# State cleared tile by tile, GpSimd scaling one tile in four, the flag and the loads in other places: one change to a graph network on one core

## The chip, the core and the metric

The kernel runs on one core of a Trainium2 chip. The core has five engines with queues of their own: TensorE (PE), VectorE (DVE), ScalarE (ACT), GpSimd (POOL) and SyncE (SP), and 16 DMA engines shared by the queues. The metric is the device time in microseconds of one execution, as the median of several.

## What is computed

A graph with N = 6250 nodes and E = 200,000 edges, sorted by target, 128 features. Two residual layers follow each other: a message network with sums by target, and an attention layer with a softmax by target.

```
edge_index = stack([src, dst])
h = maximum(layernorm(x), 0)
x = x + L0(h, edge_index, edge_attr)      # message network
h = maximum(layernorm(x), 0)
x = x + L1(h, edge_index)                 # attention

L0: m = relu(concat[h[src], h[dst], edge_attr] @ W1 + b1) @ W2 + b2
    agg = segment_sum(m, dst)
    u = relu(concat[h, agg] @ U1 + c1) @ U2 + c2
    return layernorm(h + u) * gamma + beta
L1: xl, xr = h @ Wl.T + bl, h @ Wr.T + br        (self loops added)
    e = att . leaky_relu(xl[src] + xr[dst])
    alpha = softmax of e over the edges of each target
    return elu(segment_sum(alpha * xl[src], dst) + bias)
```

## The kernel before

`gnn_program` runs the message network's edges (`edges_mlp`), a general middle part that is skipped in the fast case, and the attention (`edges_attention`). Both edge passes walk over 391 groups of 512 edges, 8 groups to a round, 49 rounds. For every group GpSimd issues four gathers (`gather_rounds`, L730) of 128 rows each from a table in memory: `tab_a` in the first pass, `tab_l` in the second. A ring of 8 group slots takes them, and a slot is free again when VectorE has added its rows (`m_sum`, L1286).

Ahead of the first pass stands the prelude (`prelude`). It loads the nodes `X` (49 tiles of 128 nodes), normalises them in 13 chunks of `CH` = 4 tiles (the last has one), and writes `tab_a`, the products of the normalised nodes with the first part of `W1`. The engines run in step `n` over the chunks:

- VectorE takes the statistics of chunk n (L578, L581) and makes the factors `rs` and `nm` of chunk n-1 (L610, L611).
- ScalarE takes the square root of chunk n (`sd`, L419), copies the turned chunk n-2 into `HT` (L423), scales chunk n-1 tile by tile into `xn`, whose buffer the profile calls m_attr_t (L431), and copies the products of chunk n-3 into the store buffer `at`, called m_pre (L438).
- TensorE turns chunk n-1 (L512) and multiplies chunk n-2 (L520).
- SyncE issues the loads, then the store of each chunk of `tab_a` (L375). There are two store buffers.

In between stands other work, hung to certain steps: GpSimd casts the edges' source and target rows (L476, L478) and reorders the target rows (`perm`, L480); TensorE turns them (`turn_rows`, L495) and VectorE takes them (`take_rows`, L567); `base` (L633) is the first target of each group's window of 32; four passes over 1568 columns and some short ones (L638 to L657) count whether the windows are as the fast path needs them; and TensorE and VectorE turn the count into `flag_i` (L551, L672). Every engine reads `flag_i` and branches (L706). GpSimd does so when all of `tab_a` and the zero rows at the tables' ends have landed, too. The products of the first five tiles for the target table `tab_b3` (L547 to L669) and their store (`store_early`, L384) are also part of the prelude; later tiles of it are made in the rounds, five ahead (`LEAD`).

The state `acc` holds 2 x 6304 sums per partition. In the rounds VectorE adds each group's window to it (L1295), and four slots into the round after the next the finished tile is used up (`tile(rnd, 2)`). `dve_tile`, `act_tile` and `pe_tile` hold this work of a round on nodes; `lead(rnd)` is the round's number up to 47.

## Time and profile before

| | us |
|---|---|
| median of 3 runs (lowest, highest) | 4053.22 (4052.76, 4057.73) |
| the profiled execution, its time | 4052.3 |
| the profiled execution, its span | 4050.5 |
| of its span busy: TensorE, VectorE | 3054.5, 2072.5 |
| of its span busy: ScalarE, GpSimd | 1780.8, 2983.4 |
| bytes moved by DMA | 455.98 MB |

The span is the stretch from the first to the last instruction that the profile shows. A row of the timeline tells an instruction's start, its length, its engine, its line, what it writes and reads, and in brackets how long the engine stood idle before it and what ended that. "issue" means that the profile shows nothing that was waited for. TensorE, weight load and matmul, has the names PEld and PE; a queue that issues DMAs has the name of its engine with a q.

### The profile page before, as it was taken

What the parts mean: (1) busy time and instruction counts of PE and PEld (TensorE: products, weight loads), DVE (VectorE), ACT (ScalarE), POOL (GpSimd) and SP (SyncE); (2) the same over time, 40 slices, a digit from 0 to 9 for tenths busy, and PEclk for the clock granted to TensorE, in tenths of its full rate; (3) what the DMA queues carried; (4) which work ended last, traced back from release to release, by engine and by line L of the source; (5) the groups of instructions that cost most, each with busy time, mean ns of one, the idle gap of its engine ahead of it and who ended that gap; (6) DMA issues with size and microseconds to landing.
All of it is one profiled execution on the core that took longest, in us unless ns stands there. A gap on an engine that the chain in (4) does not pass through costs nothing. (4 is left out here: it accounts for less than half of the span.)

```text
span 4050.5 us, 117915 instructions
## 1 busy us (share of the span) xinstructions
PE 3054.5 (75%) x30845; PEld 2211.2 (55%) x30845; DVE 2072.5 (51%) x7909; ACT 1780.8 (44%) x4395; POOL 2983.4 (74%) x3154
## 2 busy tenths in 40 slices
PE   4778878778887778788857777777777777777776
PEld 3667666666666666666634444444444444444444
DVE  5344444444444444444435555655565565556555
ACT  4333333333333333333335555555555555555555
POOL 4777777777777777777747777777777777777775
PEclk8777777877777777777768888888888888888887
DMA  6555555555555555555423333333333333333332
GB/s 163 144 145 139 145 142 143 144 141 140 143 146 137 146 141 145 138 146 137 121 65 86 85 86 85 85 85 86 85 85 85 86 86 85 85 85 86 85 85 58
DMA packets 397865, 455.98 MB, mean 113 GB/s; under 512 B 156453, under 2 KB 296963, under 8 KB 397791
## 3 DMA queue, kind: packets, MB, share of 16 engines
q1 hardware_dynamic: 297295, 249.90, 22.4%
q0 software_dynamic: 100096, 205.00, 20.4%
q8 instruction: 34, 0.56, 0.1%
q14 instruction: 40, 0.33, 0.0%
q10 hardware_dynamic: 400, 0.20, 0.0%
HBM read 434.70 MB, written 20.07 MB: 112 GB/s over the span
## 5 line engine op out<-in xcount | busy, mean ns | idle before, releaser
L730 POOL DMA_INDIRECT m_ring<-tab_a,m_idx x1564 | 1483.5, 949 | 516.5 <-issue 508.9
L730 POOL DMA_INDIRECT t_ring<-tab_l,t_idx x1564 | 1478.3, 945 | 517.1 <-issue 458.9
L1192 PE MATMUL bank<-w,m_attr_t 128*128 128x128 f32 x3128 | 733.5, 363 | 91.2 <-DVE m_hot L1276 91.0
L1909 PE MATMUL bank<-t_hot_t,t_win 96*128 96x128 bf16 x1564 | 329.3, 238 | 514.0 <-DMA t_ring<-tab_l,t_idx 506.2
L1192 PEld LDWEIGHTS bank<-w,m_attr_t 128*128 128x128 f32 x3128 | 629.6, 249 | 146.6 <-issue 107.2
L1241 ACT ACTIVATE m_hid<-m_pre 128x512 f32<-128x512 f32 x391 | 246.4, 630 | 999.9 <-DVE m_pre L1286 986.0
L1286 DVE TENSOR_TENSOR m_pre<-bank,m_ring 128x512 f32<-128x512 f32 x391 | 270.2, 691 | 784.2 <-DMA m_ring<-tab_a,m_idx 439.4
L1918 PE MATMUL bank<-t_zt,att_wn 128*128 128x512 f32 x782 | 545.4, 788 | 0.7 <-DVE t_zt L2018 0.7
L1960 ACT ACTIVATE t_z<-bank 128x512 f32<-128x512 f32 x391 | 233.5, 597 | 667.0 <-PE bank L1911 639.7
L1909 PEld LDWEIGHTS bank<-t_hot_t,t_win 96*128 96x128 bf16 x1564 | 166.3, 108 | 603.4 <-issue 581.2
L2062 DVE TENSOR_TENSOR t_old<-acc,t_shrink 128x64 f32<-128x64 f32 x391 | 88.3, 226 | 695.8 <-ACT t_shrink L1973 609.4
L1194 PE MATMUL bank<-m_win,m_hot_t 96*128 96x128 bf16 x1564 | 402.4, 257 | 0.0
L1928 PEld LDWEIGHTS bank<-t_a_edge,t_ring 128*32 128x32 f32 x12512 | 159.7, 126 | 421.7 <-issue 418.8
L1911 PE MATMUL bank<-ident,t_ring 128*128 128x128 f32 x1564 | 366.8, 311 | 0.0
L1954 ACT ACTIVATE t_a_edge<-bank 128x512 f32<-128x512 f32 x391 | 233.0, 596 | 237.6 <-PE bank L1899 227.7
L1183 PE MATMUL bank<-ident,m_ring 128*128 128x128 f32 x1564 | 306.8, 331 | 22.5 <-DMA m_win<-tab_b 22.5
L1236 ACT ACTIVATE m_attr_t<-bank 128x512 f32<-128x512 f32 x391 | 229.6, 587 | 156.5 <-PE bank L1183 155.2
L1966 ACT ACTIVATE t_a_row<-t_logit,t_den_max 128x512 f32<-128x512 f32 x391 | 278.5, 712 | 0.5 <-DVE t_den_max L2027 0.4
L1978 ACT ACTIVATE t_pen<-t_hot_t,t_big 128x512 f32<-128x512 bf16 x391 | 277.4, 710 | 0.0
L1899 PE MATMUL bank<-ident,t_a_row 128*128 128x128 f32 x1564 | 268.5, 299 | 10.8 <-ACT t_a_row L1966 2.0
L1202 PE MATMUL bank<-m_hid,m_hot 128*32 128x129 f32 x3128 | 193.6, 325 | 109.5 <-ACT m_hid L1241 69.8
L2018 DVE TENSOR_TENSOR t_zt<-bank,t_z 128x512 f32<-128x512 f32 x391 | 264.6, 677 | 11.9 <-ACT t_z L1960 11.9
(206 smaller groups left out, 5253.6 us busy)
## 6 DMA issues: line engine op xcount, KB each, us to landing
m_ring<-in_edge_attr_dram SPq DMA_DIRECT2D x390, 256.0 KB
m_row<-dst_rows SPq DMA_DIRECT2D x391, 128.0 KB
t_row<-dst_rows SPq DMA_DIRECT2D x391, 128.0 KB
m_ring<-tab_a,m_idx POOLq DMA_INDIRECT x1564
t_ring<-tab_l,t_idx POOLq DMA_INDIRECT x1564
m_win<-tab_b SPq DMA_DIRECT2D x391, 24.0 KB
t_win<-tab_r SPq DMA_DIRECT2D x391, 24.0 KB
tab_r<-n_r SPq DMA_DIRECT2D x49, 96.0 KB
```

The source lines that it names most:

```text
L730: pool.indirect_dma_start(out=r.got[u][0:rows, j, :], out_offset=None, in_=table, in_offset=bass.IndirectOffsetOnAxis(ap=r.idx[half][0:row ...
L1183: last = pe.transpose(p_attr[u % 2][:, j * P:(j + 1) * P], attr[u][:, j, :], k.ident[:])
L1192: pe.matmul(p_hid[q % 2][:, e], lhsT=attr_t[q % 2][:, e], rhs=k.w1[:, 2, :], start=True, stop=False)
L1194: last = pe.matmul(p_hid[q % 2][:, e], lhsT=hot_t[q % 2][0:3 * W, e], rhs=r.win[q][:], start=False, stop=True)
L1286: dve.tensor_tensor(pre[q % 2][:], p_hid[q % 2][:], r.got[q][:].rearrange("p j d -> p (j d)"), ALU.add).then_inc(s["m_sum"], 1)
L1899: last = pe.transpose(p_turn[:, e], a_row[q % 2][:, e], k.ident[:])
L1909: pe.matmul(p_z[q % 2][:, e], lhsT=r.win[q][:], rhs=hot_t[q % 2][0:3 * W, e], start=True, stop=False)
L1911: last = pe.matmul(p_z[q % 2][:, e], lhsT=r.got[q][:, j, :], rhs=k.ident[:], is_transpose=True, start=False, stop=True)
L1918: pe.matmul(p_e[q % 2][:], lhsT=k.att_wn[:], rhs=zt[q % 2][:], start=True, stop=True).then_inc(s["t_ep"], 1)
L1966: act.activation(a_row[q % 2][:], logit[q % 2][:], ACT.Exp, scale=-1.0, bias=den_max[q % 4][:, 1:2], accum_out=den_max[q % 4][:, 0:1]).the ...
L1978: act.activation(pen[q % 4][:], hot_t[q % 2][:], ACT.Identity, bias=big[:, 0:1], scale=-BIG).then_inc(s["t_pen"], 1)
L2018: dve.tensor_tensor(zt[q % 2][:], p_z[q % 2][:], z02[q % 2][:], ALU.max).then_inc(s["t_z"], 1)
```

## The change

Four edits, all but one in the prelude.

1. `acc` is no longer cleared in one instruction. GpSimd clears the columns behind the last tile and the first tile; in the rounds VectorE clears tile d+1 of both halves in round d, at slot 2, and the addition of slot 3 waits for it. The flag's condition on the windows (`iota_b`, `k.ahead`) is drawn to fit.
2. GpSimd scales the fourth tile of each full chunk, ScalarE the other three; TensorE waits for both. GpSimd's casts and reorderings stand between its scalings.
3. Steps are moved: the target rows are turned one step earlier, the starts `base` are made at step 9 and 10 and not 10 and 11, the count's passes stand in steps 11, 12 and 13 and not behind all, and the weights' products three or four steps later. The flag is made ahead of the products for the first target tiles.
4. SyncE issues 8 of the 18 weights ahead of the stores, the others by fives in front of the second and the third, the 11 zero rows in front of the sixth and the row table's store in front of the tenth. In the first round it issues the edge loads first and `store_early` behind them.

```
     k.tiles = -(-N // P)
     k.timely = min((k.groups - LATE - 1) // U, k.tiles)
-    k.ahead = min(k.NT + 2 - LEAD, NR)
+    k.ahead = min(k.NT - 1, NR)
...
         row_loads(sp, 1, "dst", s["s_dst"])
-        for dst, src in weights:
-            sp.dma_start(dst, src).then_inc(s["s_wt"], 16)
         sp.wait_ge(s["s_pool"], 3)
         z16 = k.zrow[:].bitcast(BF16)[:, 0:P]
         top = k.NP - W
-        for part in range(3):
-            sp.dma_start(k.tab_b3[top:k.NP, part, :], z16).then_inc(s["s_tops"], 16)
-            sp.dma_start(k.tab_r3[top:k.NP, part, :], z16).then_inc(s["s_tops"], 16)
-        for tab in (k.tab_b, k.tab_r, k.tab_a, k.tab_l):
-            sp.dma_start(tab[top:k.NP, :], k.zrow[:]).then_inc(s["s_tops"], 16)
-        sp.dma_start(k.tab_es[:, top:k.NP], k.zrow[0:H, 0:W]).then_inc(s["s_tops"], 16)
+        tops = [(tab[top:k.NP, part, :], z16) for tab in (k.tab_b3, k.tab_r3) for part in range(3)]
+        tops += [(tab[top:k.NP, :], k.zrow[:]) for tab in (k.tab_b, k.tab_r, k.tab_a, k.tab_l)]
+        tops.append((k.tab_es[:, top:k.NP], k.zrow[0:H, 0:W]))
+        for dst, src in weights[:8]:
+            sp.dma_start(dst, src).then_inc(s["s_wt"], 16)
         for c in range(NC):
-            if c == min(6, NC - 1):
+            for dst, src in weights[8 + 5 * (c - 1):8 + 5 * c if c < NC - 1 else None] if c else []:
+                sp.dma_start(dst, src).then_inc(s["s_wt"], 16)
+            if c == min(5, NC - 1):
+                for dst, src in tops:
+                    sp.dma_start(dst, src).then_inc(s["s_tops"], 16)
+            if c == min(9, NC - 1):
                 sp.wait_ge(s["s_conv"], 3)
                 sp.dma_start(k.dst_rows.rearrange("(b g) e -> g b e", g=GB), perm[:]).then_inc(s["s_permout"], 16)
             sp.wait_ge(s["a_a"], c + 1)
...
@@ first_scalar
-                for q in range(size(c)):
+                for q in range(min(size(c), CH - 1)):
...
@@ first_gpsimd
-        pool.memset(k.acc[:], 0.0).then_inc(s["s_acc"], 1)
-        pool.wait_ge(s["s_src"], n_rows)
-        pool.tensor_copy(rows_f[:, 0], rows_i[:, 0]).then_inc(s["s_conv"], 1)
-        pool.wait_ge(s["s_dst"], n_rows)
-        pool.tensor_copy(rows_f[:, 1], rows_i[:, 1]).then_inc(s["s_conv"], 1)
-        for b in range(NBLK):
-            last = pool.tensor_copy(perm[:, b, :].rearrange("g (j p) -> g j p", j=J),
-                                    rows_i[:, 1, b, :].rearrange("g (p j) -> g j p", j=J))
-        last.then_inc(s["s_conv"], 1)
+        pool.memset(k.acc[:, :, k.NT * P:], 0.0)
+        pool.memset(k.acc[:, :, 0:P], 0.0).then_inc(s["s_acc"], 1)
+
+        def scale(c):
+            if size(c) == CH:
+                i = c * CH + CH - 1
+                pool.wait_ge(s["a_nm"], c + 1)
+                after(pool, s["a_tp"], c - 1)
+                pool.tensor_scalar(xn[c % 2][:, CH - 1, :], k.X[:, i, :], rs[:, i:i + 1], nm[:, i:i + 1], ALU.mult,
+                                   ALU.add).then_inc(s["a_xp"], 1)
+
+        for c in range(max(NC, NBLK + 4)):
+            if c < NC:
+                scale(c)
+            if c == 0:
+                pool.wait_ge(s["s_src"], n_rows)
+                pool.tensor_copy(rows_f[:, 0], rows_i[:, 0]).then_inc(s["s_conv"], 1)
+            if c == 3:
+                pool.wait_ge(s["s_dst"], n_rows)
+                pool.tensor_copy(rows_f[:, 1], rows_i[:, 1]).then_inc(s["s_conv"], 1)
+            if 0 <= c - 4 < NBLK:
+                last = pool.tensor_copy(perm[:, c - 4, :].rearrange("g (j p) -> g j p", j=J),
+                                        rows_i[:, 1, c - 4, :].rearrange("g (p j) -> g j p", j=J))
+                if c - 4 == NBLK - 1:
+                    last.then_inc(s["s_conv"], 1)
...
@@ first_tensor
+                after(pe, s["a_xp"], min(c + 1, NT // CH))
...
-            if n == 10:
+            if n == 9:
...
+        pe.wait_ge(s["s_cnt"], 1)
+        pe.matmul(p_misc[:, 0:1], lhsT=k.ones[:], rhs=cnt[:, 2:3], start=True, stop=True).then_inc(s["s_flagp"], 1)
...
@@ first_vector
-            if n == 11:
+            if n == 10:
                 dve.wait_ge(s["s_conv"], 3)
...
-            if n == steps - 1:
+            if n == 11:
                 link(dve.tensor_tensor(rel, k.dst_t[:, 0:G, :],
                                        k.base[:].unsqueeze(2).to_broadcast([P, G, J]), ALU.subtract))
-            if n == steps - 1:
+            if n == 11:
                 hits = hit.rearrange("p (g j) -> p g j", j=J)
                 link(dve.tensor_scalar(hits, rel, 0.0, None, ALU.is_ge))
+            if n == 12:
                 link(dve.scalar_tensor_tensor(out=rel, in0=rel, scalar=float(W), in1=hits, op0=ALU.is_lt, op1=ALU.mult))
                 link(dve.tensor_reduce(cnt[:, 0:1], rel, mybir.AxisListType.XY, ALU.add))
+            if n == 13:
                 link(dve.tensor_tensor(hit[:, 0:G - 1], k.base[:, 1:G], k.base[:, 0:G - 1], ALU.is_ge))
...
+        dve.wait_ge(s["s_flagp"], 1)
+        dve.tensor_scalar(k.flag_i[:], p_misc[0:1, 0:1], float(E + P * (G - 1 + k.timely + k.ahead)), None, ALU.is_equal
+                          ).then_inc(s["s_flag"], 1)
...
@@ edges_mlp
+            if u == 2 and d is not None:
+                dve.tensor_scalar(k.acc[:, :, bass.ds((d + 1) * P, P)], k.ones[:].unsqueeze(1).to_broadcast([P, 2, P]),
+                                  0.0, None, ALU.mult).then_inc(s["n_clr"], 1)
...
-                store_early(sp)
                 sp.wait_ge(k.s_flag, 1)
                 with sp.If(is_fast(sp, k)):
                     def body(rnd, slots, _):
                         if isinstance(rnd, int) and rnd == 0:
                             for u in slots:
                                 load_edges(sp, u, u)
+                            store_early(sp)
                             for u in slots:
                                 load_targets(sp, u, u)
...
+                                if u == 3 and not tail and lead(rnd) is not None:
+                                    hold(dve, s["n_clr"], rnd + 1)
```

What moved on GpSimd, from its last constant of the prelude on. `m_attr_t` is `xn`, `m_ring` holds the rows and their casts. Before:

```order
L464 IOTA pm 128x1
L474 MEMSET acc 128x12608
L476 CAST m_ring<-m_ring 98x2048 [waits s_src]
L478 CAST m_ring<-m_ring 98x2048 [waits s_dst]
L480 CAST perm<-m_ring 98x512 x4
L706 TENSOR_LOAD flag_i [waits s_tops,s_flag,a_ast1,a_ast0]
```

And now:

```order
L468 IOTA pm 128x1
L478 MEMSET acc 128x2x32
L479 MEMSET acc 128x2x128
L486 TENSOR_SCALAR m_attr_t<-X,rs,nm 128x128 [waits a_nm]
L494 CAST m_ring<-m_ring 98x2048 [waits s_src]
L486 TENSOR_SCALAR m_attr_t<-X,rs,nm 128x128 [waits a_nm]
...
L497 CAST m_ring<-m_ring 98x2048 [waits s_dst]
L486 TENSOR_SCALAR m_attr_t<-X,rs,nm 128x128 [waits a_tp,a_nm]
L499 CAST perm<-m_ring 98x512
...
L731 TENSOR_LOAD flag_i [waits s_tops,s_flag,a_ast1,a_ast0]
```

The long clear is gone, the two short ones stand in its place, and each cast and reordering has a scaling in front of it that waits for VectorE's factors (a_nm).

On VectorE, from the last factors ahead of `base` to the flag. Before:

```order
L633 TENSOR_SCALAR base<-bank 128x392 [waits s_basep,s_conv]
L634 CAST base_i<-base 1x392 [waits s_chain]
...
L578 BN_STATS m_hid<-X 128x6 [waits s_x6]
L581 BN_AGGR mv<-m_hid 128x2 [waits s_chain]
...
L611 SCALAR_TENSOR_TENSOR nm<-mv,rs 128x1 [waits s_chain]
L638 TENSOR_TENSOR m_ring<-dst_t,base 128x1568
L642 TENSOR_SCALAR m_ring<-m_ring 128x1568 [waits s_chain]
L643 SCALAR_TENSOR_TENSOR m_ring<-m_ring 128x1568 [waits s_chain]
L644 TENSOR_REDUCE cnt<-m_ring 128x1 [waits s_chain]
L645 TENSOR_TENSOR m_ring<-base 128x391 [waits s_chain]
...
L672 TENSOR_SCALAR flag_i<-bank 1x1 [waits s_flagp]
```

And now:

```order
L656 TENSOR_SCALAR base<-bank 128x392 [waits s_basep,s_conv]
L657 CAST base_i<-base 1x392 [waits s_chain]
...
L600 BN_STATS m_hid<-X 128x6 [waits s_x6]
...
L661 TENSOR_TENSOR m_ring<-dst_t,base 128x1568
L665 TENSOR_SCALAR m_ring<-m_ring 128x1568 [waits s_chain]
L600 BN_STATS m_hid<-X 128x6 [waits s_x6,s_chain]
...
L667 SCALAR_TENSOR_TENSOR m_ring<-m_ring 128x1568
L668 TENSOR_REDUCE cnt<-m_ring 128x1 [waits s_chain]
...
L670 TENSOR_TENSOR m_ring<-base 128x391
...
L684 TENSOR_SCALAR flag_i<-bank 1x1 [waits s_flagp]
```

The statistics of a whole chunk and of the last tile (L600, L603) now stand between `base` and the passes over 1568 columns, which stood in one piece behind them.

On SyncE, from the end of the row loads to the first stores of the target table. Before:

```order
L317 DMA m_ring<-in_dst_dram 1x320
...
L360 DMA att<-in_L_gnn_att_dram 128x1
L365 DMA tab_b<-zrow 32x128 [waits s_pool]
...
L369 DMA tab_es<-zrow 4x32
L375 DMA tab_a<-m_pre 128x4x128 [waits a_a] x6
L373 DMA dst_rows<-perm 98x4x512 [waits s_conv]
L375 DMA tab_a<-m_pre 128x4x128 [waits a_a] x6
L375 DMA tab_a<-m_pre 128x128 [waits a_a]
L384 DMA tab_b<-n_tiles 128x4x384 [waits s_tcopy,a_lo,s_tops,s_permout]
...
L706 TENSOR_LOAD flag_i [waits s_flag,a_bst1,a_bst0]
```

And now:

```order
L366 DMA b_bc<-in_L_gnn_msg_b_dram 128x128
L377 DMA tab_a<-m_pre 128x4x128 [waits a_a]
...
L369 DMA blr_bc<-in_L_gnn_b_r_dram 128x128
L377 DMA tab_a<-m_pre 128x4x128 [waits a_a]
...
L377 DMA tab_a<-m_pre 128x4x128 [waits a_a] x3
L372 DMA tab_b<-zrow 32x128 x3
...
L377 DMA tab_a<-m_pre 128x4x128 [waits a_a] x4
L375 DMA dst_rows<-perm 98x4x512 [waits s_conv]
L377 DMA tab_a<-m_pre 128x4x128 [waits a_a] x3
...
L731 TENSOR_LOAD flag_i [waits s_tcopy,s_flag,s_tops,s_permout]
...
L1059 DMA m_row<-dst_rows 128x512
L386 DMA tab_b<-n_tiles 128x4x384 [waits a_lo]
```

The first store of `tab_a` had 29 small DMAs in front of it behind the row loads and now has 8, the last of them the row of `b_bc`; the two stores of `tab_b` stand behind the flag and the edge loads.

## Rows read from the trace of the kernel before

**Rows 1.** The page's groups: busy us, mean ns; idle before, releaser

```profile
L730 POOL DMA_INDIRECT m_ring<-tab_a,m_idx x1564 | 1483.5, 949 | 516.5 <-issue 508.9
```

**Rows 2.** Timeline of GpSimd (start, length, us): first and last gathers

```profile
69.86 1.13 POOL L730 DMA_INDIRECT m_ring<-tab_a,m_idx  x1 [40.15 <-issue]
...
2028.77 0.90 POOL L730 DMA_INDIRECT m_ring<-tab_a,m_idx  x1 [0.30 <-issue]
...
2070.43 0.94 POOL L730 DMA_INDIRECT t_ring<-tab_l,t_idx  x1 [40.77 <-DVE t_idx L716]
```

**Rows 3.** Timeline of the start

```profile
3.91 10.60 POOL L474 MEMSET acc<- 128x12608 f32 x1
...
7.39 7.16 DVE L585 TENSOR_SCALAR thirds<-thirds 128x42 f32<-128x42 f32 x1
...
14.46 1.89 POOL L476 CAST m_ring<-m_ring 98x2048 f32<-98x2048 int32 x1
...
15.01 1.55 DVE L589 SCALAR_TENSOR_TENSOR ph<-pm,ph 128x1 f32<-128x1 f32 x2
...
18.03 1.65 ACT L431 ACTIVATE m_attr_t<-X,nm,rs 128x128 f32<-128x128 f32 x4 [10.22 <-DVE nm L611]
```

**Rows 4.** Timeline: GpSimd's second cast, ScalarE's steps of chunks 2 to 5

```profile
23.58 1.89 POOL L478 CAST m_ring<-m_ring 98x2048 f32<-98x2048 int32 x1 [7.24 <-DMA m_ring<-in_dst_dram]
...
24.83 1.63 ACT L431 ACTIVATE m_attr_t<-X,nm,rs 128x128 f32<-128x128 f32 x4
...
27.46 0.60 ACT L423 ACTIVATE HT<-bank 128x512 f32<-128x512 f32 x1 [0.33 <-PE bank L512]
...
27.96 1.64 ACT L431 ACTIVATE m_attr_t<-X,nm,rs 128x128 f32<-128x128 f32 x4
...
31.09 0.30 ACT L419 ACTIVATE sd<-mv,eps 128x4 f32<-128x4 f32 x1 [1.01 <-DVE mv L581]
```

**Rows 5.** Timeline: turned target rows, window starts, count and flag

```profile
37.79 1.64 ACT L431 ACTIVATE m_attr_t<-X,nm,rs 128x128 f32<-128x128 f32 x4
...
43.79 0.30 ACT L419 ACTIVATE sd<-mv,eps 128x4 f32<-128x4 f32 x1 [1.00 <-DVE mv L581]
...
46.94 0.30 ACT L419 ACTIVATE sd<-mv,eps 128x4 f32<-128x4 f32 x1 [0.35 <-DVE mv L581]
...
52.51 0.56 DVE L633 TENSOR_SCALAR base<-bank 128x392 f32<-128x392 f32 x1 [3.90 <-PE bank L541]
...
58.02 1.79 DVE L643 SCALAR_TENSOR_TENSOR m_ring<-m_ring 128x1568 f32<-128x1568 f32 x1
...
58.14 0.48 ACT L431 ACTIVATE m_attr_t<-X,nm,rs 128x128 f32<-128x128 f32 x1
...
61.67 0.57 DVE L645 TENSOR_TENSOR m_ring<-base 128x391 f32<-128x391 f32 x1
...
62.04 0.28 ACT L438 ACTIVATE m_pre<-bank 128x128 f32<-128x128 f32 x1 [0.46 <-DMA tab_a<-m_pre]
...
64.26 0.16 DVE L657 TENSOR_TENSOR cnt<-cnt 128x1 f32<-128x1 f32 x1
...
67.92 0.14 DVE L672 TENSOR_SCALAR flag_i<-bank 1x1 int32<-1x1 f32 x1
```

**Rows 6.** Timeline of SyncE's queue: one issue

```profile
26.27 0.43 SPq L365 DMA_DIRECT2D tab_b<-zrow  x1
```

**Rows 7.** DMA view up to 72 us: issues, KB, median us to landing

```profile
tab_a<-m_pre SPq DMA_DIRECT2D x1, 64.0 KB, 1.8
```

**Rows 8.** Timeline of the first round

```profile
72.17 0.35 SPq L1029 DMA_DIRECT2D m_ring<-in_edge_attr_dram  x1
...
92.17 0.69 DVE L1286 TENSOR_TENSOR m_pre<-bank,m_ring 128x512 f32<-128x512 f32 x1 [3.34 <-PE bank L1194]
```

**Rows 9.** Timeline of a later round: a gather and a copy onto the state

```profile
158.96 0.95 POOL L730 DMA_INDIRECT m_ring<-tab_a,m_idx  x1 [0.30 <-issue]
...
159.01 0.22 DVE L963 COPY acc<-ones 128x128 f32<-128x128 f32 x1
```

More of the change, by code:

```diff
@@ L398, in general_rows_vector @@
     def general_rows_vector(dve):
+        dve.memset(k.acc[:, :, P:], 0.0).then_inc(s["z_acc"], 1)
+        dve.wait_ge(s["z_acc"], 1)
         for c in range(NC):
@@ L468, in first_gpsimd @@
         iota(k.iota_t[:], [[P, k.timely]], 0, P)
-        iota(k.iota_b[:], [[P, k.ahead]], 0, (LEAD - 2) * P - W)
+        iota(k.iota_b[:], [[P, k.ahead]], 0, 2 * P - W)
         iota(k.iota_q[:], [[1, H], [0, W]], 0)
@@ L501, in first_tensor @@
                 pe.wait_ge(s["s_w1"], 16)
-            if n == 6:
+            if n == 9:
                 pe.wait_ge(s["s_wt"], n_wt)
@@ L528, in first_tensor @@
                     turn_rows(b)
-            if n == 7:
+            if n == 6:
                 for b in range(min(2, NBLK)):
                     turn_rows(NBLK + b)
-            if n == 8:
+            if n == 7:
                 for b in range(2, NBLK):
                     turn_rows(NBLK + b)
+            if n == 11:
                 pe.wait_ge(s["s_w2t"], 1)
@@ L538, in first_tensor @@
                           ).then_inc(s["s_w2p"], 1)
-            if n == 10:
+            if n == 9:
                 pe.wait_ge(s["s_tcopy"], 2 * NBLK)
@@ L549, in first_tensor @@
             last.then_inc(s["a_bp"], 1)
-        pe.wait_ge(s["s_cnt"], 1)
-        pe.matmul(p_misc[:, 0:1], lhsT=k.ones[:], rhs=cnt[:, 2:3], start=True, stop=True).then_inc(s["s_flagp"], 1)
         pe.wait_ge(s["s_flag"], 1)
@@ L620, in first_vector @@
                 idx_ready(dve)
-            if n == 8:
+            if n == 7:
                 for b in range(min(2, NBLK)):
                     take_rows(NBLK + b)
-            if n == 9:
+            if n == 8:
                 for b in range(2, NBLK):
                     take_rows(NBLK + b)
+            if n == 13:
                 dve.wait_ge(s["s_w2p"], 1)
@@ L629, in first_vector @@
                 dve.tensor_copy(k.b2u[:], p_w[:, P:P + 1])
-            if n == 11:
+            if n == 10:
                 dve.wait_ge(s["s_conv"], 3)
@@ L810, in edges_mlp @@
                        "n_hp n_ht n_d n_zb n_rows n_hi n_zt n_m n_mc n_r1 n_mid n_lo n_lout n_rout n_hb n_bp n_bb n_bhi "
-                       "n_br n_bmid n_blo n_bst")
+                       "n_br n_bmid n_blo n_bst n_clr")
         def sb(name, shape, dt):
```

8 lines of the change are left out of this document (3 added, 5 removed).

## The prediction

> **What bounds the kernel now.** I read the page first, then the timeline of GpSimd, then that of all engines up to the first gather. The page's costliest group is the first edge pass's gathers [rows 1]: 1564 of 949 ns, with about 0.33 us of idle time before each (516.5 / 1564, the prelude's 40.1 among it). GpSimd's timeline gives both ends of the first pass: the first gather starts at 69.86, the last at 2028.77 [rows 2]. That is (2028.77 - 69.86) / 1563 = 1.253 us a gather, so almost nothing but gather and issue. So between 70 and 2029 us the clock of the kernel is GpSimd's gather stream. Between the passes 40.8 us go to the last tiles and the switch, and the second pass is again a gather stream, from 2070.43 [rows 2]. Nothing in the rounds can shorten this unless it makes a gather cheaper. What can move the end is the first gather's start: the 69.86 us of the prelude.
>
> **The start (removes the full clear).** GpSimd clears the state in one instruction of 10.60 us at 3.91. VectorE's small comparison of a 128x42 tile starts at 7.39 and takes 7.16 us, until 14.55, when the clear ends at 14.51 [rows 3]. Then two tiny VectorE operations take 1.55 us at 15.01, while GpSimd's cast from 14.46 runs 1.89 us to 16.35 [rows 3]. ScalarE's first scaling waits for the result and starts at 18.03, after 10.22 us idle [rows 3]. In the change GpSimd clears 2x32 and 2x128 columns, 320 of 12,608: 0.27 us at the same rate. The comparison then takes about 0.2 us (gain 7.0), and the cast stands behind the first GpSimd scaling, so the pair takes about 0.35 us (gain 1.2). VectorE's chain ends at about 9.8, and the first scaling starts at **9.9 instead of 18.03: -8.1 us**. Data is no limit there as far as the rows show: the cast at 14.46 waited for no load.
>
> The Trainium skill, "SBUF — State Buffer", section "SBUF: two separate sides", calls the port pair of VectorE and GpSimd an exclusive lock held for a whole instruction; the two stalls above agree with it (7.16 and 1.55 us). The next paragraphs use the stalls only.
>
> **The scaling (GpSimd takes tile 4 of 4).** ScalarE's four scalings take 1.63 us [rows 4], three take 1.22: 0.41 us less in each of 12 chunks, 4.9 us if ScalarE sets the pace. It does not everywhere. From the first scaling to the end of the third chunk's, before took 26.46 - 18.03 = 8.4 us; TensorE's work between them does not shrink, so I take 0.8 and not 1.2 off: the end is at 17.5. From there to the square root of chunk 5 (chunks count from 0) at 31.09, which waited 1.01 us for VectorE [rows 4], it is a chain of 4.6 us over TensorE's turned rows and VectorE's statistics. It is kept: 22.1. Gain so far 9.0.
>
> **What takes some back.** GpSimd works in order. Its second cast waits for the target rows, which came at 23.58 [rows 4] and are issued at the same time as before, so the fourth tile of chunk 4 can be scaled only behind the cast, from 25.5 to 25.9; ScalarE's three are done at about 24.5. From the end of one chunk's scaling to the start of the next (TensorE turns it, ScalarE copies it at 27.46, the next begins 0.5 later) the rows give 27.96 - 26.46 = 1.5 us [rows 4]. So ScalarE ends its part of chunk 5 at 25.9 + 1.5 + 1.3 = 28.7, some 1.1 us later than without the cast. GpSimd's own scaling is bounded by 0.12 us (128 columns at the cast's rate, 1.89 us for 2048 [rows 4]) and the 0.48 us of one on ScalarE (1.64 for four overlapping); I take 0.4, hidden beside ScalarE's 1.22.
>
> **Steps moved forward.** The turning of the target rows, and the window starts built on them, stand one chunk earlier, so this chain ends about 2.8 us sooner relative to the chunks. VectorE waited 3.90 us for those starts, until 52.51 [rows 5]. Step by step: before, from the end of a scaling (37.79 + 1.64 = 39.43) over the turned target rows to the next statistics (the square root at 43.79) took 4.4 us, and the next round of the same 3.15, to 46.94 [rows 5]. That makes 28.7 + 4.4 = 33.1, and 36.2. The starts came 52.51 - 46.94 = 5.6 us later, now 5.6 - 0.4 = 5.2: 41.4. Their four operations take 1.5 us (0.56 the first), and the statistics of chunk 11 1.3: 44.2. Here the change also costs: the checks of 1568 columns (1.79 us [rows 5], three of that length and one of 0.98) stood behind all statistics, and now stand between them. 44.2 plus normal factors, two of the four checks and the last statistics gives 48.1; plus the other two (58.02 to 61.67, 3.65 us [rows 5]) and the last factors 52.4. The last tile is scaled by 52.9, where before had 58.14 + 0.48 = 58.62 [rows 5]. From there to the last product before took 62.32 - 58.62 = 3.7 us, with 0.46 us of waiting for a store [rows 5]; without that 3.3: **56.2 instead of 62.32**.
>
> **The flag.** It was written at 67.92, behind the products for the first target tiles [rows 5], and the first gather followed it by 1.8 us (69.86 - 68.06). Now it comes before them. The short checks (61.67 to 64.42, 2.75 us [rows 5]) plus two copies of 0.35 us give the count at 52.4 + 3.1 = 55.5; TensorE's last products end shortly before 56.2, and the flag stands at about 56.8. What is late next is not the flag but the last store: issued at 56.2, 1.8 us to landing [rows 7], so 58.1. GpSimd waits for the stores too. Plus the same 1.8 us: **first gather at 59.9; with 0.2 for GpSimd's scaling 60.1. Gain 9.8 us.**
>
> **SyncE's queue.** An issue costs 0.43 us and a short gap [rows 6], 0.47 together. Weights: 8 before the first store (to 21.2, where the first store is due at about 18), then five and five (2.35 us each) in gaps of about 3 us. The 11 zero rows (5.1 us) stand behind the fifth store and make the sixth 2 us late; its buffer is needed again two chunks later, some 5 us. The row table's store stands in front of the tenth. The last weight is out at about 27 and is needed at 36. All hidden, cost 0; if a buffer is late, up to 2 us.
>
> **The first round.** The store of the first target tiles now stands behind 16 edge loads. Before: loads from 72.17, and 20.0 us later, at 92.17, the first slot is freed [rows 8]. After: loads from about 58.6, and between them and the target tiles the two stores, which drain behind 3 MB of loads; I allow 7 us: slot freed at 58.6 + 27 = 85.6. GpSimd has 32 gathers (40 us) before it needs it, at 100. Nothing is paid, and 14 us of cover are left.
>
> **The clear in the rounds.** 48 new VectorE operations of 2x128 columns: twice the copy of 128 columns of 0.22 us [rows 9] makes 0.44, with one start instead of two 0.4, an estimate. VectorE has room: GpSimd's even pace [rows 2] shows that it waits for nobody, and its ring of eight groups is 40 us of cover. The question is whether it lengthens gathers. All VectorE work together lengthens them by at most 949 - 940 = 9 ns on average, 14 us in the pass; one more operation a round is a small part of that. The nearest row is that copy, onto the same tile, at 159.01 inside a gather of 0.95 us begun at 158.96 [rows 9]: 0.01 over the 0.94 of the one at 2070.43 [rows 2], when VectorE does little. Bounds: 0 and the clear's full length, 48 x 0.4 = 19 us. I take 1 us by the copy's row.
>
> The Trainium skill has a rule against this edit: the same page, box "The DVE blocks DMA trap (SWDGE)", says that while VectorE runs an operation in a two-port mode, GpSimd cannot write descriptors. By that rule the sum would be +9 us instead of -8.8; the copy's row speaks against it.
>
> **Sum.** 4052.3 (profiled execution; 1.8 us outside its span) - 9.8 + 1.0 = 4043.5. That execution is 0.9 us below the median of the three runs, so **4044.4 us** is what I forecast for the median.
>
> **Rivals.** (1) The prelude stays bound by VectorE and the casts. GpSimd's second cast and its four pieces of row reordering now run while VectorE works, and its two-input operations may wait as the pair at 15.01 did. With 1.9 + 2 us of that, and GpSimd's scalings waiting in turn, the gain is 9.8 - 3.9 = 5.9 and the time 4048.3. For it: both stalls of [rows 3]. Against: each piece starts right behind factors just made, and the next are due some 2.4 us later. (2) ScalarE's shorter step counts fully and the target rows come earlier: the 1.1 us and 0.8 us come back, gain 11.7, time 4042.5 or somewhat less. (3) Slower: each clear holds its gather for its whole length, at slot 2 of each round. 48 x 0.4 = 19 against 9.8: 4062. It decides from 0.2 us a clear, since 48 x 0.2 eats the gain. Against it, the row at 159.01. (4) The change doesn't do what it says: the loads of nodes and indices are the bound behind the clear, VectorE waits for node tiles instead, and only the flag's move stays: 67.92 + 1.8 against 64.1 + 1.8, about 3.7 us, 4050.4. For it, the target rows that came only at 23.58; against, nothing waited for a load at 14.46.
>
> **How the numbers follow.** Forecast 54%, (1) 20%, (2) 16%, (3) 4%, (4) 6%. 0.2% is 8.1 us, about what a measurement of this kernel can tell from no change, and the limit is 4045.1. The forecast lies only 0.7 us below it, and with a spread of 1.5 us of its own, 37 of its 54 points lie under it; with (2) that is 53% faster. The rest of it, (1) and (4) are within 0.2%: 43%. Slower, (3): 4%. The range goes from (2) to (4): 4041 to 4050.
>
> **What would show it.** In the changed profile: the small comparison at 7.4 takes 0.2 us; the first scaling starts at 9.9 (rival 4: at 12 or later, behind a load); GpSimd's second cast at about 23.6; the last product before the first gather ends near 56.2; the flag before the last store has landed; the first gather at 60.1; the last one at about 2020, with the mean of a gather at 949 to 950 ns (rival 3: 960 or more). The gap between the passes stays 40.8 us. I am wrong if the first gather starts after 62, or if (last - first) / 1563 differs from 1.253 by more than 0.002.

## The result

The changed kernel takes 4043.52 us (median of 14, 4041.48 to 4049.44) against 4052.75 for the kernel before on the same chip (14, 4050.82 to 4057.73): ratio 0.9978, interval 0.9970 to 0.9986, a gain of 9.2 us. The forecast was 4044.4.

The profiled execution of the changed kernel is the slowest of its 14: 4049.44 us, span 4047.5. The page's group of the first pass's gathers, to be read beside [rows 1], and GpSimd's timeline with the ends of the pass, beside [rows 2]:

```profile
L755 POOL DMA_INDIRECT m_ring<-tab_a,m_idx x1564 | 1486.3, 950 | 485.3 <-issue 478.3
```

```profile
62.09 1.15 POOL L755 DMA_INDIRECT m_ring<-tab_a,m_idx  x1 [8.83 <-issue]
...
2023.91 0.90 POOL L755 DMA_INDIRECT m_ring<-tab_a,m_idx  x1 [0.30 <-issue]
2064.89 0.95 POOL L755 DMA_INDIRECT t_ring<-tab_l,t_idx  x1 [40.08 <-DVE t_idx L741]
```

The first gather starts 7.8 us earlier (62.09 against 69.86). The pass takes 1961.8 us to its last gather where it took 1958.9, and the stretch from 2064.89 to the end 1982.6 where it took 1980.1, though that code is unchanged. More on these 3 + 2.5 us below.

The timeline of the start, beside [rows 3]:

```profile
3.90 0.15 POOL L478 MEMSET acc<- 128x64 f32 x1
...
7.64 0.15 DVE L607 TENSOR_SCALAR thirds<-thirds 128x42 f32<-128x42 f32 x1
...
8.24 0.35 DVE L611 SCALAR_TENSOR_TENSOR ph<-pm,ph 128x1 f32<-128x1 f32 x2
...
10.07 1.26 ACT L435 ACTIVATE m_attr_t<-X,nm,rs 128x128 f32<-128x128 f32 x3 [2.02 <-DVE nm L633]
10.14 0.45 POOL L486 TENSOR_SCALAR m_attr_t<-X,rs,nm 128x128 f32<-128x128 f32 x1 [5.84 <-DVE nm L633]
```

The comparison is down from 7.16 to 0.15 us, the pair from 1.55 to 0.35, and the first scaling starts 8.0 us earlier. The timeline of the steps behind it, beside [rows 4] and [rows 5] (left out are the rows between):

```profile
22.37 0.43 SPq L377 DMA_DIRECT2D tab_a<-m_pre  x1
...
23.51 0.30 ACT L423 ACTIVATE sd<-mv,eps 128x4 f32<-128x4 f32 x1 [2.12 <-DVE mv L603]
...
24.49 1.89 POOL L497 CAST m_ring<-m_ring 98x2048 f32<-98x2048 int32 x1 [7.70 <-DMA m_ring<-in_dst_dram]
24.71 1.77 DVE L741 COPY m_idx<-src_t 128x16 int32<-128x16 int32 x2
...
25.34 0.43 SPq L377 DMA_DIRECT2D tab_a<-m_pre  x1
...
26.43 0.60 ACT L442 ACTIVATE m_pre<-bank 128x512 f32<-128x512 f32 x1 [0.99 <-DMA tab_a<-m_pre]
...
32.52 0.60 ACT L442 ACTIVATE m_pre<-bank 128x512 f32<-128x512 f32 x1 [2.88 <-DMA tab_a<-m_pre]
...
35.31 0.29 ACT L423 ACTIVATE sd<-mv,eps 128x4 f32<-128x4 f32 x1
...
44.51 0.57 DVE L656 TENSOR_SCALAR base<-bank 128x392 f32<-128x392 f32 x1 [2.07 <-PE bank L563]
...
47.49 1.78 DVE L661 TENSOR_TENSOR m_ring<-dst_t,base 128x1568 f32<-128x1568 f32 x1
...
47.68 1.93 POOL L486 TENSOR_SCALAR m_attr_t<-X,rs,nm 128x128 f32<-128x128 f32 x1 [4.68 <-DVE nm L633]
...
58.54 0.28 ACT L442 ACTIVATE m_pre<-bank 128x128 f32<-128x128 f32 x1 [0.95 <-DMA tab_a<-m_pre]
58.56 0.15 DVE L684 TENSOR_SCALAR flag_i<-bank 1x1 int32<-1x1 f32 x1 [0.48 <-PE bank L566]
58.85 0.34 SPq L377 DMA_DIRECT2D tab_a<-m_pre  x1
```

Three things are new. ScalarE waits for stores to land (0.99 and 2.88 us). A scaling on GpSimd that takes 0.45 us elsewhere takes 1.93 beside a long two-input operation of VectorE. And TensorE runs a part of the prelude at the lower of its two clocks. The last is seen in the view of busy times for 27.0 to 57.8 us, in the kernel before, in the changed kernel, and in its second profile, that of the control run below. After the busy time of each engine come the granted TensorE clock as a share of full speed, the DMA share and GB/s:

```profile
27.00:57.80 30.80, 20.46 (x156) 17.70 (x156) 20.80 (x101) 25.30 (x64) 2.71 (x3) 1.00 0.40 98
```

```profile
27.00:57.80 30.80, 21.28 (x132) 18.45 (x132) 22.79 (x93) 19.31 (x48) 10.14 (x11) 0.83 0.39 109
```

```profile
27.00:57.80 30.80, 21.39 (x121) 19.10 (x120) 19.24 (x70) 17.98 (x44) 9.36 (x11) 0.78 0.37 101
```

In the kernel before the clock is full (2.4 GHz) over the whole stretch. In the changed kernel it is 0.50 (1.2 GHz) from 27.7 to 30.4 us and from 47.9 to 54.6. Before the first fall TensorE stood idle for 2.97 us, and during the second for 3.83, from the end of its products at 45.88 to 49.70.

### The profile page after: what moved, and what is told of

Same layout as the page of the kernel before. It is cut to its first block and busy times, and to the rows that moved or that the text cites. A ratio compares the mean times of both kernels' runs of the same rounds, so it can differ in the third digit from the quotient of the medians.

```text
span 4047.5 us, 118065 instructions
## 1 busy us (share of the span) xinstructions
PE 3061.0 (76%) x30845; PEld 2214.9 (55%) x30845; DVE 2082.8 (51%) x7957; ACT 1781.0 (44%) x4383; POOL 2987.0 (74%) x3167
## 3 DMA queue, kind: packets, MB, share of 16 engines
q1 hardware_dynamic: 297295, 249.90, 22.1%
```

## The experiments

The runs were made in three groups, each with runs of the kernel before on the same chip. One group (the changed kernel again, the clear alone, the flag alone, the weights late) was on a chip that grants TensorE a mean clock of 0.66 to 0.67 of full speed instead of 0.80; there every kernel takes about 6090 us. The others were on one further chip of the usual kind.

### The price of the clears in the rounds

Take the clears out of the rounds. GpSimd clears four tiles behind each of its scalings (the pieces kernel):

```
-            if u == 2 and d is not None:
-                dve.tensor_scalar(k.acc[:, :, bass.ds((d + 1) * P, P)], ..., 0.0, None, ALU.mult).then_inc(s["n_clr"], 1)
...
             if c < NC:
                 scale(c)
+            if c < NC - 1:
+                last = pool.memset(k.acc[:, :, P + c * CH * P:P + (c + 1) * CH * P], 0.0)
```

> The changed kernel with no clear in the rounds: GpSimd clears four tiles of both halves (2x512 columns, 0.86 us) behind each of its 12 scalings. Shows what the clears in the rounds cost. Theory A (about 0.02 us a clear): the pace of the pass is lower by at most 1 us over 1563 gathers than the changed kernel's in the same call. Rival B: the pass is 3 us or more shorter. The pieces may stall VectorE's two-input operations for up to 0.86 us each in the prelude; if they do, the first gather is 1 to 5 us later.

Measured: 4050.97 against 4060.46 us, ratio 0.9977 (0.9968 to 0.9987), 9.5 us less. In the same group every clear was made four times:

```
+                for again in range(4):
+                    dve.tensor_scalar(k.acc[:, :, bass.ds((d + 1) * P, P)], ...).then_inc(s["n_clr"], 1)
+                    hold(dve, s["n_clr"], 4 * d + again + 1)
```

> The changed kernel with each clear in the rounds done four times one after the other: 144 more VectorE operations of 2x128 columns. Theory A: time as the changed kernel, up to 3 us more. Rival F (the page's rule: a clear holds the gather beside it for its whole length, 0.3 to 0.4 us): 144 x 0.35 = 50 us more. Rival B: three times the 3 us, 9 us more.

Measured: 4053.28, 2.3 us over the pieces kernel. Its trace has the 192 clears (the view of one line: least, median and longest duration in ns):

```profile
L979 DVE TENSOR_SCALAR acc<-ones x192: 283/294/544, 88.1 to 1969.5; 128x256 f32 x176, 128x256 f32<-128x256 f32 x16
```

They are 56 us of VectorE's time, and the medians differ by 2.3 us, 12 ns each, with overlapping intervals. That no clear holds a gather for its length was settled, but not whether the change's 48 cost 0 or 3 us. So the changed kernel, the pieces kernel, and one whose clear writes 2x1 columns only were run side by side:

```
-  k.acc[:, :, bass.ds((d + 1) * P, P)], k.ones[:].unsqueeze(1).to_broadcast([P, 2, P])
+  k.acc[:, :, bass.ds((d + 1) * P, 1)], k.ones[:, 0:1].unsqueeze(1).to_broadcast([P, 2, 1])
```

> The changed kernel again, beside the others of this call. The first gather should start at 62.1 us as in its first profile. Theory A (the clears in the rounds cost some 2 to 3 us): its last gather of the first pass stands at 1.255 us a gather, the second pass with what follows takes 1982 to 1983 us, and the time is 2 to 4 us above that of the pieces kernel below. Theory B (the two are the same, and the difference between runs on different chips misled): its pace is 1.2535, and both times lie within 1 us.

> The changed kernel without clears in the rounds; GpSimd clears four tiles behind each of its scalings. Measured once before: first gather 62.59, pace 1.2535, from the first gather of the second pass to the end 1980.7. Both theories expect 62.6 and 1.2535 again; it is the measure for the other three. Time against the kernel before: 9 to 10 us less.

> The pieces kernel, with an instruction of 2x1 columns put where the clear of 2x128 stood in each round: the same number of instructions in the loop as in the changed kernel, but almost no work. Theory W (the cost is the clear's work on VectorE beside the gathers): pace 1.2535 and rest of the second pass 1980.7, as without clears; time as the pieces kernel within 1 us. Theory P (the cost comes with one instruction and its wait more in the program, not with its work; for it speaks that the second pass, whose code is the same in all, is also 2 to 3 us longer wherever the clears are in the rounds): pace 1.255 and rest 1983, as the changed kernel, time 2 to 4 us above the pieces kernel.

Measured, with the kernel before at 4059.25: the changed kernel 4050.39 (ratio 0.9977, 0.9968 to 0.9986), the pieces kernel 4050.84, the tiny clear 4052.47. By the medians of 11 runs the clears cost -0.5 us, which is nothing. The tiny clear, which does less, is 1.6 us above the pieces kernel, outside the 1 us of theory W and below the 2 to 4 of theory P: a difference of that size says nothing here. So theory B holds for the time. The profiles say something else: the changed kernel's pace is again 1.2555 us a gather, as theory A had it. GpSimd's timeline of the changed kernel, then of the pieces kernel's first gather, then the page's groups of both passes in each:

```profile
64.24 1.28 POOL L755 DMA_INDIRECT m_ring<-tab_a,m_idx  x1 [9.47 <-issue]
...
2026.55 0.90 POOL L755 DMA_INDIRECT m_ring<-tab_a,m_idx  x1 [0.30 <-issue]
2068.02 0.95 POOL L755 DMA_INDIRECT t_ring<-tab_l,t_idx  x1 [40.57 <-DVE t_idx L741]
```

```profile
64.03 1.15 POOL L759 DMA_INDIRECT m_ring<-tab_a,m_idx  x1 [7.96 <-issue]
```

```profile
L755 POOL DMA_INDIRECT t_ring<-tab_l,t_idx x1564 | 1481.7, 947 | 517.1 <-issue 458.8
L755 POOL DMA_INDIRECT m_ring<-tab_a,m_idx x1564 | 1486.6, 951 | 486.1 <-issue 480.9
```

```profile
L759 POOL DMA_INDIRECT t_ring<-tab_l,t_idx x1564 | 1477.7, 945 | 517.1 <-issue 455.3
L759 POOL DMA_INDIRECT m_ring<-tab_a,m_idx x1564 | 1483.0, 948 | 484.4 <-issue 479.2
```

In the profiled executions the gathers of the pieces kernel take 3.6 us less in the first pass and 4.0 in the second, where no kernel clears anything by tiles. But its profiled execution (4045.47) is 5.4 us below its own median and the fastest of its 11, and that of the changed kernel (4053.53) 3.1 above its median and the slowest. The earlier group's pieces kernel was the same (4046.03, the fastest of 10). So a difference of 3 to 4 us a pass, seen in the profiled executions alone, isn't in the time of the others.

Two profiles of the changed kernel differ by 2.2 us at the first gather (62.09, 64.24), and here TensorE's clock shows why. The products of chunk 5 in the first profile, then the same products and the square root of chunk 9 in the second:

```profile
35.48 1.06 PE L541 MATMUL bank<-w,HT 128*128 128x128 f32 x8
```

```profile
36.08 1.91 PE L541 MATMUL bank<-w,HT 128*128 128x128 f32 x8
40.81 0.30 ACT L423 ACTIVATE sd<-mv,eps 128x4 f32<-128x4 f32 x1 [2.19 <-DVE mv L603]
```

In the second profile the granted clock is 0.50 from 34.9 to 38.0 us, and in the first it is full there. The square root of chunk 8 is only 0.2 us later in the second (35.49), that of chunk 9 1.5 us (40.81 against 39.31). The rest comes at the end, where the products of chunk 10 take 1.91 us instead of 1.28 and the last ones 1.75 instead of 1.28.

The tiny clear's profile has long gathers as well (951 and 947 ns), so there it isn't the clear's work that lengthens them; what does is open.

### What the start alone brings

The kernel before with nothing but the clear changed:

```
-        pool.memset(k.acc[:], 0.0).then_inc(s["s_acc"], 1)
+        pool.memset(k.acc[:, :, k.NT * P:], 0.0)
+        pool.memset(k.acc[:, :, 0:P], 0.0).then_inc(s["s_acc"], 1)
```

> The kernel before with only the first edit: short clears on GpSimd, a tile cleared per round by VectorE. Theory A: the 7.16 us and 1.2 us stalls of VectorE vanish, the first scaling starts at about 10, and the first gather comes 7 to 8 us earlier, at 62 to 63; time 6 to 8 us less than before. Rival C (the clear hid other waits: loads of nodes and of the target rows are next): the first gather comes 3 to 5 us earlier, time 3 to 5 us less.

Measured, on the chip of the low clock: the first gather at 70.57, no earlier than before (69.86, on the first chip). The first scaling starts at 12.62, and the timeline shows where the rest goes:

```profile
10.68 1.89 POOL L479 CAST m_ring<-m_ring 98x2048 f32<-98x2048 int32 x1 [6.40 <-DMA m_ring<-in_src_dram]
10.72 1.87 DVE L614 SCALAR_TENSOR_TENSOR nm<-mv,rs 128x4 f32<-128x4 f32 x1
...
30.88 12.45 SPq L375 DMA_DIRECT2D tab_a<-m_pre  x6
...
33.32 0.60 ACT L440 ACTIVATE m_pre<-bank 128x512 f32<-128x512 f32 x1 [4.24 <-DMA tab_a<-m_pre]
...
43.95 0.30 ACT L421 ACTIVATE sd<-mv,eps 128x4 f32<-128x4 f32 x1 [1.01 <-DVE mv L584]
```

GpSimd's cast now meets the first factors, a product of 128x4 that takes 1.87 us. Then SyncE is the bound: its first store is the next in the queue behind 29 small transfers and goes out at 30.88, and ScalarE, whose store buffer it holds, waits 4.24 us. The square root of [rows 5] at 43.79 stands at 43.95. Its time, 10 us above the kernel before, is dealt with under the chip of the low clock. Does the new order on SyncE give the gain back? The same kernel with `first_sync` of the change, and the steps that wait for all weights put behind them:

```
-            if n == 6:
+            if n == 9:
                 pe.wait_ge(s["s_wt"], n_wt)
...
-            if n == 7:
+            if n == 10:
                 dve.wait_ge(s["s_wt"], n_wt)
```

> The kernel before with two edits of the change: the state cleared tile by tile, and the order of weights and zero rows on SyncE (with the steps that wait for all weights moved behind them). ScalarE scales all, the flag stays behind the target tiles, target rows and counts stand as before. Theory Q (clearing alone gave nothing at the first gather, 70.57, because the first store stood behind 29 small transfers on SyncE, so the two edits need each other): first scaling at 12.6 or earlier, no wait of 4 us for a store at step 5, first gather at about 65, which is 69.9 less 5. Rival R (the count and the starts behind it bound that kernel anyway): first gather at 69 to 70.5 again. The time is the kernel before's less 2 to 3 us by Q, and plus 1 to 3 by R.

Measured: 4056.99 against 4059.25, 2.3 us less (ratio 0.9994, 0.9985 to 1.0003, so it is not told from no change), first gather at 69.08. Its timeline:

```profile
23.48 0.30 ACT L423 ACTIVATE sd<-mv,eps 128x4 f32<-128x4 f32 x1 [1.03 <-DVE mv L587]
...
32.59 0.60 ACT L442 ACTIVATE m_pre<-bank 128x512 f32<-128x512 f32 x1 [1.37 <-DMA tab_a<-m_pre]
...
40.20 0.30 ACT L423 ACTIVATE sd<-mv,eps 128x4 f32<-128x4 f32 x1 [1.45 <-DVE mv L587]
...
51.46 0.57 DVE L640 TENSOR_SCALAR base<-bank 128x392 f32<-128x392 f32 x1 [4.81 <-PE bank L547]
...
67.13 0.14 DVE L679 TENSOR_SCALAR flag_i<-bank 1x1 int32<-1x1 f32 x1
```

Theory Q is right up to chunk 5 (23.48 against 31.09, the 7.6 us are there) and rival R from then on: 3.6 us are left at 40.20 (43.79 before), 1.1 at the window starts (51.46, 52.51 before), 0.8 at the flag. VectorE waits 4.81 us for the starts. The first gather is as rival R said, and the time as theory Q. The early start is eaten by stores, by the second cast, by the place of the target rows, starts and weights in the order of steps, and by TensorE's clock; no run tells their shares. The granted clock is 0.50 in three stretches (about 27 to 30, 37 to 40 and 47 to 50.5 us) where the kernel before has it full, and again from about 57, so that the products for the first target tiles, on which the flag waits, take 2.50 us instead of 1.38.

The flag alone, in the kernel before, ahead of the products for the first target tiles:

> The kernel before with the flag alone moved ahead of the products for the first target tiles; all else, also the store of those tiles ahead of the edge loads, as before. The count is ready at 64.4 in before and the flag would be at 65.1, the last store lands at 64.2. Theory A: the first gather at 65.1 + 1.8 = 66.9, 3.0 us earlier, time 3 us less. Rival C (the short products and the edge loads matter too): less than 1 us.

Measured, at the low clock: first gather at 66.94, 2.9 us earlier than [rows 2]; 6086.91 against 6090.12 us, 3.2 us less by the medians, with a ratio (0.9999, 0.9989 to 1.0008) that doesn't tell it from no change. The change with all four tiles of a chunk scaled by ScalarE, as before:

```
-                for q in range(min(size(c), CH - 1)):
+                for q in range(size(c)):
```

> The changed kernel with ScalarE scaling all four tiles again and GpSimd none. Theory A: ScalarE's step is 0.4 us longer, but the chain over TensorE and VectorE sets much of the stretch; first gather 1 to 2.5 us later than 62.1. Rival G (GpSimd's scaling, stuck behind its casts and VectorE's long operations, costs what it gives): within 0.5 us of the changed kernel. Full worth by count, 12 x 0.41 = 4.9 us, would show ScalarE to be the bound.

Measured: first gather at 62.44, inside what the changed kernel shows in two profiles (62.09, 64.24); the time, 4054.78, is 3.8 us above the pieces kernel of its group, and its gain over the kernel before 5.7 us where the changed kernel has 8.9 on the same chip. By the medians GpSimd's scaling brings some 3 us. The intervals overlap (0.9977 to 0.9995 here, 0.9968 to 0.9986 for the change), though the times themselves hardly do (4052.99 to 4055.98 against 4046.03 to 4053.26 of the pieces kernel), and the first gather doesn't show the 3 us. By these medians the parts add up: 2.3 for the clear with SyncE's order, 3.2 for the flag (on the other chip) and 3 to 4 for the scaling, against 8.9. None of them is told surely by itself, and the moved steps had no run of their own.

### SyncE's queue

All weights behind the first store, three in front of each later one:

```
-        for dst, src in weights[:8]:
-            sp.dma_start(dst, src).then_inc(s["s_wt"], 16)
...
-  weights[8 + 5 * (c - 1):8 + 5 * c if c < NC - 1 else None] if c else []
+  weights[3 * (c - 1):3 * c if c < NC - 1 else None] if c else []
```

> The changed kernel with no weights ahead of the first store of the table and three, not five, in front of each later one. In the changed kernel ScalarE waited 0.99, 2.88 and 0.95 us for stores of its two buffers. Theory D (SyncE's queue was not free: the stores stand behind weights, and this costs about 1 to 2 us of the prelude): the first two waits go, chunk 8's square root comes 1 to 2 us earlier than 35.31, the first gather at 60 to 61, time 1 to 2 us less than the changed kernel. Rival E (the chain over the turned target rows sets that stretch): the waits go and the first gather stays at 62.1 within 0.3.

Measured, at the low clock. Theory D's first half came true: ScalarE no longer waits for a store in this stretch, and the square roots of chunks 8 and 9 come at 32.47 and 34.97, where the changed kernel on the same chip has 34.62 and 39.34. Chunk 9 here, then there:

```profile
34.97 0.30 ACT L421 ACTIVATE sd<-mv,eps 128x4 f32<-128x4 f32 x1
```

```profile
39.34 0.30 ACT L423 ACTIVATE sd<-mv,eps 128x4 f32<-128x4 f32 x1 [2.31 <-DVE mv L603]
```

Of these 4.4 us, 1.0 is there at chunk 5 already (21.95 against 23.00). The other 3.4 come with the waits for stores (0.55 and 2.49 us in the changed kernel there) and with TensorE's clock, whose mean from 27 to 38 us is 0.94 here and 0.54 there. But the first gather is at 64.66, 1.9 us later than the changed kernel there (62.76), which is within what two profiles of one kernel differ by, and the median is 4.8 us above the changed kernel's. The timeline behind chunk 9:

```profile
39.81 0.45 SPq L367 DMA_DIRECT2D att<-in_L_gnn_att_dram  x1
...
41.95 0.48 PE L522 MATMUL bank<-ident,wl 128*128 128x128 f32 x1 [5.95 <-DMA att<-in_L_gnn_att_dram]
```

The last weight goes out 12 us later than in the change (27.81), and TensorE, in order, waits 5.95 us for it with its chunk behind. So the late weights give back all that the early stores bring. The change's five at a time is the better side of this trade; three at a time with TensorE's wait moved further back was not run. Next, the target rows ahead of the last two loads of nodes, so that the second cast comes early:

```
+            if n == 4:
+                row_loads(sp, 1, "dst", s["s_dst"])
...
-        row_loads(sp, 1, "dst", s["s_dst"])
```

> The changed kernel with the target rows' loads issued two node loads earlier, in front of tiles 24 and up. GpSimd's second cast started at 24.49, behind that load, and held a scaling. Theory H (that cast is on the path): the cast at 20 to 21, the stretch behind it 1 us shorter, first gather 1 us earlier. Rival E: the later node loads are late instead, or the chain of turned rows sets the time: within 0.3 us or later.

Measured: 4053.8, 2.8 us above the pieces kernel of its group, first gather at 64.73. The cast does come early:

```profile
17.54 1.89 POOL L498 CAST m_ring<-m_ring 98x2048 f32<-98x2048 int32 x1 [0.89 <-DMA m_ring<-in_dst_dram]
...
33.52 0.60 ACT L443 ACTIVATE m_pre<-bank 128x512 f32<-128x512 f32 x1 [4.49 <-DMA tab_a<-m_pre]
```

It frees nothing, since ScalarE then waits 4.49 us for a store. Up to there the store, and not the cast, is the tighter limit.

### The chip of the low clock

> The changed kernel once more, nothing altered. Its first trace has the first gather at 62.09 and the last of the first pass at 2023.91 (1.2552 us a gather; before 1.2533), a span 3.0 us shorter than before's, and is the slowest of its 14 runs; their median is 9.2 us shorter. Theory A (the prelude carries the whole gain, the pass's pace only varies): first gather again 62.1, pace 1.253 to 1.254, time 9 us less than before in the median. Rival B (the clears in the rounds cost about 3 us in the pass in every run): pace 1.255 again, with the median's gain coming from somewhere behind the first pass.

Measured: 6099.87 against 6090.12, ratio 1.0018 (1.0009 to 1.0028): there the change is 10 us slower, and so is the clear alone (6099.94); with the weights late it is 6104.65. Theories A and B can't be told apart there, since GpSimd no longer sets the pace of the pass. What TensorE waited for between 500 and 2000 us (us in total, times, longest), in the changed kernel there, then in the kernel with the flag alone on the same chip, whose rounds are those of the kernel before:

```profile
PE bank L1230 <- DVE acc L1325: 313.6, 20, 16.1
PE bank L1220 <- issue: 199.2, 112, 6.9
```

```profile
PE bank L1202 <- DVE acc L1295: 317.9, 20, 16.0
```

On that chip TensorE stands still for up to 16 us and starts its matmuls singly, microseconds apart, with nothing to wait for; GpSimd is no longer the bound, and stands idle 1822 us before the gathers of the first pass. Both kernels there have these stops in nearly the same size, while in the kernel before on the usual chip no wait of that stretch is over 6.3 us: they belong to the chip and not to the change. The first gather comes early there too (62.76), but it buys nothing. Where the 10 us come from isn't settled. The three kernels that lose 10 to 15 us there are those with the clears in the rounds, and the flag alone, without them, loses nothing; but the second pass, whose code is the same and has no clears, takes 2688.9 us (3408.96 to the end) against 2678.8 with the flag alone. The pieces kernel, which would separate the two, was not run there.

## Why the prediction was right, step by step

| step | forecast | measured |
|---|---|---|
| comparison; first scaling starts | 0.2; 9.9 | 0.15; 10.07 |
| third chunk's scaling ends | 17.5 | 17.95 |
| square root of chunk 5 | 22.1 | 23.51 |
| second cast | 23.6 | 24.49 |
| the two square roots for 33.1 and 36.2 (chunks 8, 9) | 33.1, 36.2 | 35.31, 39.31 |
| window starts | 41.4 | 44.51 |
| square roots of chunks 11 and 12 | 44.2, 48.1 | 47.35, 51.01 |
| last product; flag | 56.2; 56.8 | 58.82; 58.56 |
| first gather | 60.1 | 62.09, 64.24 |
| 48 clears | +1 | -0.5 |
| time | 4044.4 | 4043.52 |

**The start** went as forecast, by stalls that are gone: the trace's own numbers gave it to 0.2 us. Some of the stalls came back elsewhere: two copies of 128x16 integers take 1.77 us beside the second cast (0.25 before), and GpSimd's scaling 1.93 and 1.92 beside VectorE's count. That was rival 1's mechanism; it struck in these three places, and the count's two-input operations ran at their old length (1.78). The Trainium skill, "SBUF — State Buffer", section "SBUF: two separate sides", calls the port pair that VectorE and GpSimd share an exclusive lock, which the one that starts first holds for its whole instruction. These three rows agree with it.

**SyncE's queue** is one of two steps that failed. "All hidden, cost 0; if a buffer is late, up to 2 us" took 1.8 us to landing from [rows 7], the row of the last store, which stands alone in its queue. In the middle of the weights a store takes far longer, and what in them lengthens it no run shows. The view of the store's line from 22 to 30 us (the issues at 22.37, 25.34 and 28.29):

```profile
  ACT m_pre L442: 3.9, 2
...
DMA to landing us min/median/max: 4.0/5.4/7.1
```

The first landed after 4.0 us, and the copy of chunk 2 waited for it until 26.43; the second after 7.1, and the copy of chunk 3 waited until 32.52. Before, the six stores from 31.3 to 42.8 us, behind all weights, had a median of 2.3. The chain is 2.2 late at chunk 8 and 3.1 at chunk 9, and it stays 3.1 late to the window starts. With the weights late these waits are gone, and both square roots come before their forecast (32.47 and 34.97). The moved steps behind them cost what was forecast (2.8 us from the starts to the next square root where 2.8 was said, 3.7 to the last where 3.9 was).

**TensorE's clock** is the other. The forecast kept TensorE's work and the chains over it as the kernel before has them, at the full clock, and had no term for a fall. The chain is 1.4 us late already at chunk 5, before any wait for a store. Ahead of it the turning of chunk 2 and the products of chunk 1 take 1.11 and 1.84 us, and in the second profile, where they take 0.66 and 1.06, chunk 5 is on time (22.24 against 22.1). The rows show the granted clock as full in that stretch, so for chunk 5 only the durations are shown. Later the clock itself stands at 0.50 (27.7 to 30.4 and 47.9 to 54.6 us, and 24.8 to 31.1, 34.9 to 38.0 and 51.9 to 58.3 in the second profile). TensorE has new stops ahead of these falls or in them: until 26.91 behind GpSimd's scaling, which stood behind the second cast, until 49.70 behind the window starts and GpSimd's long scaling, and in the second profile until 35.17 behind a store. So the two steps can't be parted fully.

**The flag** stands 0.29 us before the last store is issued, as forecast the store is late next, and the first gather follows that issue by 3.2 us where 1.8 + 1.8 = 3.6 was said.

**The clears** were priced at 1 us against a bound of 19. They cost nothing that the times can tell, and four times as many 2.3 by the medians. The trace doesn't name the mode in which VectorE runs them, but a clear of 256 columns takes 0.294 us, as long as a two-input operation of 128 (0.29 at L628). The Trainium skill's box "The DVE blocks DMA trap (SWDGE)" on the same page says that GpSimd can't write descriptors while VectorE runs an operation in a two-port mode. If each of the 192 clears was in that mode and held a gather for its full 0.294 us, that would make 56 us, an estimate: the runs show 2.3 for this operation.

**So the first gather was 2 to 4 us later than forecast**, outside the bound of 62 that I had set. The pace of the gathers crossed the other bound in both profiles too (1.2552 and 1.2555 against 1.253 plus 0.002), and still the time came out 0.9 us below the forecast. Of the gain of 9.2 us (8.9 on the second chip) the first gather accounts for 7.8 or 5.6, by which profile one takes against 69.86, the only profile of the kernel before. The rest was not found: the profiled executions, 5.9 and 3.1 us above their medians, are not those that gave the gain, and the others left no trace. The mechanism was right, but that the total is right to 0.9 us is partly luck: it rests on an error of 2 to 4 us that something unseen made good.

## What to carry to other kernels

Take away one long stall at the start of a pipelined prelude and expect each queue behind it to take its share: the clear alone brought the first gather no earlier, with SyncE's order the time fell by 2 us, which is within the noise, and with all parts by 9. Look at the granted clock as well: here TensorE got its work sooner, stood idle more in between, and then took 1.91 us for what had taken 1.06. Take the landing time of a store from a store with the same neighbours in its queue, not from the last one. And where a change is worth a few us, compare medians and controls on the same chip: one profile of a kernel here is off by 3 to 6 us either way.

## What the runs showed that I had not expected

- A store of 256 KB takes 4.0 and 7.1 us from issue to landing among small weight transfers, and 2.3 behind them; the last one of 64 KB took 1.8 [rows 7].
- TensorE's eight products of a chunk take 1.06 us at the full granted clock and 1.91 at 0.50. The kernel before keeps the full clock from 27.0 to 57.8 us (1.00), the changed kernel has 0.83 and 0.78 there, and the matmuls that it slows account for nearly all of the 2.2 us between the first gathers of its two profiles.
- A 128x128 scaling on GpSimd takes 0.45 us, and 1.93 when it starts 0.19 us behind a two-input operation of 1.78 us on VectorE; a product of 128x4 on VectorE takes 0.16 and, 0.04 us behind a cast of 1.89 us on GpSimd, 1.87.
- One chip grants a mean TensorE clock of 0.66 to 0.67 with stops of up to 16 us, makes the kernel take half as long again (6090 us against 4053 and 4060 on two others), and turns a gain of 9 us into a loss of 10.
- The profiled execution of a kernel can be the slowest or the fastest of its runs, by up to 5.9 us, and the same way for the same kernel twice.
